# A convolution step ahead of the second pair's sums, and a bias made on GpSimd

## What is computed

```python
# block 0: bottleneck with a deformable 3 x 3 convolution
out = relu(group_norm(conv(x, w1)))                 # 256 -> 64 channels, 32 groups of 2
om = conv(out, w_off, pad=1) + b_off                # 27 rows: x and y offsets, mask
sampled = bilinear_sample(out, py, px) * sigmoid(om[:, 18:])
out = relu(group_norm(einsum(sampled, w2)))         # groups of 2 channels
x = relu(group_norm(conv(out, w3)) + x)             # 64 -> 256, groups of 8

# block 1: three convolutions on inputs rounded to 16 bits, weights to powers of two
h = shift_conv(x, w1)
h = relu(bn(shift_conv(h, peg_w, pad=1) + peg_b))
h = relu(bn(shift_conv(h, w2, pad=1)))
out = relu(bn(shift_conv(h, w3)) + x)
```

## Time and profile before

| what | us |
|---|---|
| median of 3 runs | 90.41 |
| the three runs | 89.57, 90.41, 90.43 |
| the profiled execution | 90.49 |
| its span, first to last instruction | 88.7 |
| mean granted TensorE clock in it | 0.990 |
| TensorE matmuls busy | 75.2 |
| VectorE busy | 65.4 |
| ScalarE busy | 50.1 |
| GpSimd busy | 5.0 |

### The profile page before, as it was taken

How to read it: one execution, slowest core, us unless ns; L and a number is a source line. 1 busy time by engine, 2 the same in 40 slices (tenths; PEclk the granted TensorE clock), 3 DMA queues, 4 the chain that set the end, 5 groups by cost and what they waited for, 6 DMA issues and landing times.

```text
span 88.7 us, 2177 instructions
## 1 busy us (share of the span) xinstructions
PE 75.2 (85%) x893; PEld 51.6 (58%) x893; DVE 65.4 (74%) x176; ACT 50.1 (56%) x89; POOL 5.0 (6%) x10
## 2 busy tenths in 40 slices
PE   5988999996899898999999999899589887779600
PEld 1333666475698797888988897345233374555400
DVE  0424539999999789999897725899896784967850
ACT  4203165679974999996868003906672254732660
POOL 7600110000000000000003100000000000000000
PEclk9999999999999999999999999999999999999995
DMA  1999800000000000000000000000000000000076
GB/s 30 326 317 313 346 12 0 7 0 0 0 7 0 0 7 0 4 11 0 0 7 0 0 0 7 0 0 0 0 0 0 0 0 0 0 7 4 5 258 211
DMA packets 3290, 4.17 MB, mean 47 GB/s; under 512 B 272, under 2 KB 2704, under 8 KB 3280
## 3 DMA queue, kind: packets, MB, share of 16 engines
q1 hardware_dynamic: 3008, 3.76, 13.0%
q10 hardware_dynamic: 272, 0.26, 0.9%
HBM read 2.98 MB, written 1.05 MB: 45 GB/s over the span
## 4 chain that ended last, share of the span: by engine, by line
PE 43%; DVE 31%; ACT 10%; DMA 6%; issue 4%; SPq 2%; DVEq 0%; ACTq 0%
PE acc L492 15%; PE slot L479 10%; DVE g_rows L926 9%; DMA x_sb<-x 6%; PE acc L624 4%; DVE g_cols L1028 3%; PE acc L603 3%; PE slot L407 3%; ACT g_cols L728 2%; PE slot L528 2%; ACT g_cols L826 2%; DVE g_cols L1074 2%; ACT pad L785 2%; PE slot L564 2%; DVE g_cols L1166 2%
## 5 line engine op out<-in xcount | busy, mean ns | idle before, releaser
L926 DVE TENSOR_TENSOR g_rows<-hats 128x2304 f32<-128x2304 f32 (+1 forms) x12 | 20.6, 1753 | 0.1
L728 ACT ACTIVATE g_cols<-slot 128x768 f32<-128x768 f32 x24 | 17.8, 829 | 3.7 <-PE slot L479 3.7
L492 PE MATMUL acc<-g_cols,v_sb 128*64 128x128 f32 x288 | 17.7, 276 | 0.0
L492 PEld LDWEIGHTS acc<-g_cols,v_sb 128*64 128x64 f32 x288 | 15.5, 137 | 1.1 <-issue 0.3
L370 PE MATMUL slot<-zeros 128*128 128x512 bf16 x54 | 15.0, 412 | 1.0 <-DVE zeros L845 1.0
L479 PE MATMUL slot<-consts_sb,g_rows 64*128 64x64 f32 x288 | 11.8, 226 | 2.1 <-DVE g_rows L926 1.7
L479 PEld LDWEIGHTS slot<-consts_sb,g_rows 64*128 64x128 f32 x288 | 10.3, 140 | 3.9 <-DVE g_rows L926 2.6
L370 PEld LDWEIGHTS slot<-zeros 128*128 128x128 bf16 x54 | 5.5, 109 | 6.9 <-issue 2.1
L785 ACT ACTIVATE pad<-g_cols 64x256 bf16<-64x256 int8 x8 | 3.3, 417 | 4.9 <-DVE g_cols L1074 4.8
L857 DVE BATCH_NORM_STATS2 stats<-acc 128x6 f32<-128x256 f32 x4 | 1.7, 430 | 4.1 <-PE acc L382 2.5
L407 PE MATMUL slot<-feat,woff_sb 128*64 128x256 f32 x36 | 4.7, 385 | 0.0
(11 more groups left out here) (141 smaller groups left out, 118.1 us busy)
## 6 DMA issues: line engine op xcount, KB each, us to landing
x_sb<-x SPq DMA_DIRECT2D x3, 256.0 KB, 4.5
out<-g_cols SPq DMA_DIRECT2D x3, 256.0 KB, 2.3
wq_sb<-wq SPq DMA_DIRECT2D x1, 484.5 KB, 6.3
woff_sb<-woff SPq DMA_DIRECT2D x1, 288.0 KB, 5.6
w_sb<-w SPq DMA_DIRECT2D x1, 288.0 KB, 5.5
x_sb<-x ACTq DMA_DIRECT2D x1, 256.0 KB, 2.9
w_sb<-w SPq DMA_DIRECT2D x1, 256.0 KB, 6.4
out<-g_cols SPq DMA_DIRECT2D x2, 128.0 KB, 1.8
```

Of the source, the lines that this page charges most:

```text
L492: mm = nc.tensor.matmul(acc[b2][rows(h), at:at + P], v_sb[:, B2 * h + b2, q, k, :], g_cols[t][h][:, NQ * k + q, :], start=(k == 0 and q == ...
L728: nc.scalar.activation(dst.rearrange("p k (r n) -> p k r n", r=HALVES), src.rearrange("p r (k n) -> p k r n", k=per), ACT.Copy).then_inc(g ...
L926: tt(g_rows[i % 3][:, taps], hats[:, t, h, 1, taps].unsqueeze(3).to_broadcast(shape), hats[:, t, h, 0, taps].unsqueeze(2).to_broadcast(sha ...
```

## The change

On TensorE the three idle matmuls before the second pair's sums are taken out. The first of the five steps of the first pair's offset convolution is put ahead of these sums, the other four behind them. In the second pair's convolution the turn of the first pair's offsets stands behind the first step instead of the second.

At the end of block 0 the bias of the second pair is made by two instructions on GpSimd instead of VectorE. The normalisation of the second pair multiplies by the scale only. The residual is added and the pieces' maxima are taken without the bias. The bias is added in the relu: on ScalarE in three instructions, one for each piece (a bias is one value per partition and piece), and on VectorE for the fourth piece. The overall maximum becomes: the first pair's four maxima first (in largest(0), ahead of that pair's relu), and at the end one operation that adds the bias to the second pair's four maxima and takes the greatest of them and of the first. The two kernels compute the same.

The diff, cut to its core:

```diff
             pair_sums(1, 0)
             conv1(1)
-            idle(IDLE[2], spare)
-            pair_sums(2, 1)
...
             pe.wait_ge(woff_in, 16)
-            for b2 in range(B2):
-                pe.wait_ge(feat_ready, b2 + 1)
-                for s in range(TAPS_A):
-                    mm = om_step(b2, s)
-                    if b2 == 1 and s == 1:
-                        pe.wait_ge(consts_in, 16)
-                        om_turn(0)
-                mm.then_inc(om_done, 1)
+            pe.wait_ge(feat_ready, 1)
+            for s in range(TAPS_A):
+                mm = om_step(0, s)
+                if s == 0:
+                    pair_sums(2, 1)
+            mm.then_inc(om_done, 1)
+            pe.wait_ge(feat_ready, 2)
+            for s in range(TAPS_A):
+                mm = om_step(1, s)
+                if s == 0:
+                    pe.wait_ge(consts_in, 16)
+                    om_turn(0)
+            mm.then_inc(om_done, 1)
+            pe.wait_ge(w2_in, 16)
...
+            pool.wait_ge(gn_ready, 11)
+            nc.gpsimd.tensor_tensor(dev_sb[:, 1, :], rstd[:, 1, :], mean_gamma[:, 1, :], ALU.mult).then_inc(dev_ready, 1)
+            pool.wait_ge(dev_ready, 1)
+            nc.gpsimd.tensor_tensor(gn_bias[:, 1, :], vec[:, V_GN3B:V_GN3B + CH * HALVES], dev_sb[:, 1, :], ALU.subtract
+                                    ).then_inc(gn_ready, 1)
...
-                a.wait_ge(gn_ready, 2 * (5 + b2))
+                a.wait_ge(gn_ready, 2 * (5 + b2) - b2)
                 for i in pieces3:
                     c, h = i // HALVES, i % HALVES
+                    bias = gn_bias[:, b2, i:i + 1] if b2 == 0 else zero_sb[:, 0:1]
...
-            def relu0(b2):
+            def relu0(b2, pieces3=(0, 1, 2)):
 
                 a.wait_ge(sum_ready, 4 * b2 + 4)
-                nc.scalar.activation(flat(y0[:, 0, b2]), flat(y0[:, 0, b2]), ACT.Relu).then_inc(relu_ready, 1)
+                if b2 == 0:
+                    nc.scalar.activation(flat(y0[:, 0, b2]), flat(y0[:, 0, b2]), ACT.Relu).then_inc(relu_ready, 1)
+                    return
+                a.wait_ge(gn_ready, 12)
+                for i in pieces3:
+                    piece = y0[:, i // HALVES, b2, i % HALVES, :]
+                    nc.scalar.activation(piece, piece, ACT.Relu, bias=gn_bias[:, b2, i:i + 1]).then_inc(relu_ready, 1)
...
                 tt(gn_scale[:, b2, :], rstd[:, b2, :], vec[:, V_GN3S:V_GN3S + CH * HALVES], ALU.mult
                    ).then_inc(gn_ready, 1)
+                if b2 == 1:
+                    return
...
                 dve.wait_ge(sum_ready, 4 * b2 + 4)
-                if b2 == B2 - 1:
-                    nc.vector.tensor_reduce(mx[:, 1, 0:1], piece_max[:].rearrange("p b i -> p (b i)"), AX_X, ALU.max
-                                            ).then_inc(max_ready, 1)
-
-                return ts(flat(y0[:, 1, b2]), flat(y0[:, 1, b2]), 0.0, None, ALU.max)
+                if b2 == 0:
+                    nc.vector.tensor_reduce(mx[:, 1, 1:2], piece_max[:, 0, :], AX_X, ALU.max)
+                    return ts(flat(y0[:, 1, b2]), flat(y0[:, 1, b2]), 0.0, None, ALU.max)
+                dve.wait_ge(gn_ready, 12)
+                nc.vector.tensor_tensor_reduce(unused[:, 0:CH * HALVES], piece_max[:, 1, :], gn_bias[:, 1, :], 1.0,
+                                               mx[:, 1, 1:2], ALU.add, ALU.max, mx[:, 1, 0:1]).then_inc(max_ready, 1)
+
+                return ts(y0[:, 1, b2, 1, :], y0[:, 1, b2, 1, :], gn_bias[:, b2, 3:4], 0.0, ALU.add, ALU.max)
```

More of the change, by code:

```diff
@@ L233, in build @@
         mean_done = sem("mean_done")
+        dev_ready = sem("dev_ready")
         var_ready = sem("var_ready")
@@ L420, in om_turn @@
                 mm.then_inc(omt_done, 1)
-            pe.wait_ge(woff_in, 16)
-            for b2 in range(B2):
-                pe.wait_ge(feat_ready, b2 + 1)
-                for s in range(TAPS_A):
-                    mm = om_step(b2, s)
-                    if b2 == 1 and s == 1:
-                        pe.wait_ge(consts_in, 16)
-                        om_turn(0)
-                mm.then_inc(om_done, 1)
             v_banks = [small[0], small[1], acc[0], acc[1]]
-            pe.wait_ge(w2_in, 16)
             def make_v(i):
@@ L452, in make_last_v @@
                                         w2_sb[rows(h), BANK:TAPS * CB], start=True, stop=True)
+            pe.wait_ge(woff_in, 16)
+            pe.wait_ge(feat_ready, 1)
[12 more added lines that the diff above has]
+            pe.wait_ge(w2_in, 16)
             for i in range(4):
@@ L746, in norm3 @@
             def norm3(b2, pieces3=(0, 1, 2)):
-                a.wait_ge(gn_ready, 2 * (5 + b2))
+                a.wait_ge(gn_ready, 2 * (5 + b2) - b2)
                 for i in pieces3:
                     c, h = i // HALVES, i % HALVES
+                    bias = gn_bias[:, b2, i:i + 1] if b2 == 0 else zero_sb[:, 0:1]
                     nc.scalar.activation(y0[:, c, b2, h, :], conv3_out(c, h, b2),
-                                         ACT.Identity, bias=gn_bias[:, b2, i:i + 1], scale=gn_scale[:, b2, i:i + 1]
+                                         ACT.Identity, bias=bias, scale=gn_scale[:, b2, i:i + 1]
                                          ).then_inc(norm3_ready, 1)
-            def relu0(b2):
+            def relu0(b2, pieces3=(0, 1, 2)):
                 a.wait_ge(sum_ready, 4 * b2 + 4)
-                nc.scalar.activation(flat(y0[:, 0, b2]), flat(y0[:, 0, b2]), ACT.Relu).then_inc(relu_ready, 1)
+                if b2 == 0:
[5 more added lines that the diff above has]
+                    nc.scalar.activation(piece, piece, ACT.Relu, bias=gn_bias[:, b2, i:i + 1]).then_inc(relu_ready, 1)
             def square4(b2):
@@ L1013, in norm3 @@
             def norm3(b2):
-                dve.wait_ge(gn_ready, 2 * (5 + b2))
-                ts(y0[:, 1, b2, 1, :], conv3_out(1, 1, b2), gn_scale[:, b2, 3:4],
-                   gn_bias[:, b2, 3:4], ALU.mult, ALU.add).then_inc(half_read, 1)
+                dve.wait_ge(gn_ready, 2 * (5 + b2) - b2)
+                if b2 == 0:
+                    ts(y0[:, 1, b2, 1, :], conv3_out(1, 1, b2), gn_scale[:, b2, 3:4],
+                       gn_bias[:, b2, 3:4], ALU.mult, ALU.add).then_inc(half_read, 1)
+                else:
+                    ts(y0[:, 1, b2, 1, :], conv3_out(1, 1, b2), gn_scale[:, b2, 3:4], None, ALU.mult
+                       ).then_inc(half_read, 1)
             def add_residual(b2, order):
@@ L1091, in _ @@
             whole(flat(quot[:, 0, 0]), 1)
-            dve.wait_ge(relu_ready, 2)
+            dve.wait_ge(relu_ready, 3)
             quotient(1, flat(quot[:, 0, 1]), flat(y0[:, 0, 1]))
+            dve.wait_ge(relu_ready, 4)
             quotient(1, flat(quot[:, 1, 1]), flat(y0[:, 1, 1]))
```

## The result

| | before | changed |
|---|---|---|
| median of 20 runs each, us | 90.41 (89.57 to 91.20) | 90.90 (90.18 to 94.33) |
| ratio | | 1.0048, 95% interval 1.0025 to 1.0071 |

The changed kernel is slower by 0.5%, 0.43 us by the ratio (90.41 x 0.0048). The forecast was a gain of 0.15 us, and the median of 90.90 lies just above the end of its range, 90.8. The change is smaller than the 1% that the chances speak of, but clear of no change, and on the other side. The ratios in this document, e13's excepted, leave out executions in which TensorE's clock was visibly disturbed, while the medians and ranges hold all; so for small differences the ratio counts.

What follows compares the result with a forecast made beforehand. The prediction took handovers spread over all engines as the bound, with ScalarE, led by TensorE's v products, late in the middle. Terms -0.02 and -0.13 gave -0.15 us, from the 90.41 median to 90.26, so 90.3; range 89.5 to 90.8.

Steps and rivals of the forecast that it cites:

- the 1% that the chances speak of: About 0.9 us, taken as what a measurement tells from no change; chances 0.10 faster, 0.86 within, 0.04 slower.
- part one: TensorE's start: three idle matmuls out, one offset convolution step ahead of the second pair's sums; -0.02 us, bounds -0.32 and +0.2.
- part two: Block 0's tail: second pair's bias moved to GpSimd and the relu; -0.14 up to the spread, -0.13 us after the relus.
- The reading of the middle: Sampling section: ScalarE, led by TensorE's v products, is late and VectorE has slack, so the end moves by the smaller gain.
- a change of 0.15: Offset convolution on TensorE: changing from a step to a full-array operation costs 0.15 us, perhaps no more than chance.
- The turn's new place: Second pair's convolution: turn 0.45 earlier but waiting 0.12, the other step 0.43 behind it; v at 15.07 instead of 15.09.
- the rival of the convolution's gain in full: Middle: sampling products pace it, so the convolution's 0.32 us arrives in full; -0.46 in all, 89.95 us, chance 0.20.
- the extra maximum: Tail, VectorE ahead of the scale: a maximum over the first pair's four values adds 0.07 us.
- the accumulating maximum: Tail, VectorE: the final maximum becomes an operation with accumulator and read-out, 0.22 instead of 0.16; +0.06 us, bounds 0 and +0.19.
- GpSimd late or in the way: Tail: bias late, +0.16 us net (90.6), or VectorE's four residual sums stretched, 0.4 us (90.7); chance 0.10.
- the nearer row: Tail: GpSimd's 256-column copy, 0.40 us, used to size its two bias instructions; twice that fits the 2.1 us cover.
- Weights late: Start: the offset convolution's weights land late and hold step 0 and all behind it; up to +0.54 us, 90.95, chance 0.10.

Runs made afterwards that it cites:

- e13: The changed kernel with the three idle matmuls put back behind the second pair's first convolution: 91.26 us, ratio 1.0109 to the kernel before.
- e1: The changed kernel again, as it is, for another profile: 90.87 us, ratio 1.0062 to the kernel before.
- e2: Only TensorE's part of the diff (idle matmuls out, step 0 ahead of the sums, turn behind one step) on the kernel before: 91.11 us, ratio 1.0053.
- e4: The kernel before with only the three idle matmuls ahead of the second pair's sums taken out: 90.38 us, ratio 0.9973.
- e10: Part one with the convolution's weights issued ahead of the second pair's x, and three idle matmuls ahead of that pair's first convolution: 91.35 us, ratio 1.0119 to before.
- e5: The kernel before, unchanged, as an experiment of its own: 90.43 us, ratio 1.0018.
- e9: The kernel before without its three idle matmuls, convolution weights issued ahead of the second pair's x, three idle matmuls ahead of its first convolution: 91.60 us, ratio 1.0138.
- e3: The diff without TensorE's part (bias on GpSimd and in the relu, start as before) on the kernel before: 90.27 us, ratio 0.9976.
- e8: Part two with the three idle matmuls taken out and the order of before: 90.24 us, ratio 0.9986 to the kernel before.
- e11: Part two alone once more, the same kernel as e3: 90.16 us, ratio 0.9949 to the kernel before.
- e14: The changed kernel a third time, as it is: 90.72 us, ratio 1.0033 to the kernel before.
- e6: Part one with the turn behind two steps of the second pair, as before: 90.88 us, ratio 1.0038 to the kernel before.
- e7: The kernel before without the three idle matmuls and with the turn behind one step, sums ahead of the whole convolution: 90.89 us, ratio 1.0020.
- e12: Part two without the three idle matmuls, order of before, once more (same kernel as e8): 91.34 us, ratio 0.9981 to the kernel before.

## Why the prediction was wrong

**The step that failed** is in part one: "The sums are a full-array operation too. They now start at 8.89 + 0.43 + 0.15 = 9.47 instead of 9.36, 0.11 later; bounds 0 (the 0.15 may be no more than chance) and 0.2." The sum on the left is nearly right: the sums start 0.63 behind the features in it and 0.73 in e1 and 0.72 in e2 (that e1's 9.51 is so near to 9.47 is in part luck, its features came 0.06 earlier). What is wrong is the 9.36 to which it is compared, and so the bound of 0.2: against e4, with the features at the same moment, e2's sums are 0.73 later, and v 0.63. So part one, forecast at -0.02 with +0.2 as the worst, cost 0.48 us (1.0053). The change puts the second pair's sums behind two things that they don't need, the first pair's features and step 0. What this costs depends on how far the moments lie behind the features. The working took 0.46 for it, from one execution, and never named it as a number that a load's landing sets.

Two sums describe the profiles of full clock in which neither x nor the weights held TensorE otherwise:

- old order: v starts 0.06 + 5.73 = 5.79 behind the second pair's moments;
- new order: step 0 starts 0.14 behind the first pair's features, the sums 0.59 behind step 0, and v 5.63 behind the sums, 6.36 in all behind the features. Where the moments come later than step 0, as in e10, it is 0.06 + 5.63 behind them.

| execution | features ready | moments ready | v by the sum | v in the trace |
|---|---|---|---|---|
| before | 8.84 | 9.30 | 15.09 | 15.09 |
| e5, old order | 8.73 | 8.77 | 14.56 | 14.56 |
| e4, old order | 9.33 | 9.26 | 15.05 | 15.05 |
| e9, old order, late x | 9.36 | 9.89 | 15.68 | 15.68 |
| e1, new order | 8.78 | 8.67 | 15.14 | 15.13 |
| e2, new order | 9.33 | 9.21 | 15.69 | 15.68 |
| e10, new order, late x | 9.36 | 10.15 | 15.84 | 15.84 |

The other profiles with a full clock there (e3, e8, e11, e13, e14) follow the same two sums to 0.01. The two are equal when the moments come 6.36 - 5.79 = 0.57 behind the features. Even the recorded execution, at 0.46, would have lost 0.1 us. And from 0.67 on, where the moments are later than step 0, the new order gains no more than 5.79 - 5.69 = 0.10. Of the thirteen other profiles with the loads in their old places two have late x, e6 at 0.50 and the disturbed one of the result. In the remaining eleven the moments come from 0.12 ahead to 0.04 behind, so part one costs 0.53 to 0.69 at v. The end follows v one for one: the span is v's start plus 73.6 in all profiles without part two that had their clock (before, e2, e4, e5, e6, e7, e9, e10), and plus 73.4 in those with it (e1, e3, e8, e11, e14). From these the changed kernel should lose about 0.6 - 0.2 = 0.4 us; measured were 0.43, 0.56 and 0.30 (the three ratios by 90.4).

**Right in part one.** A step of 0.43 and a change of 0.15 (together 0.58 to 0.59 in e1 and e2). The features of the first pair to step 0 took 0.14 instead of the 0.05 assumed, which is small. The reading of the middle holds. VectorE's chain did come 0.3 earlier relative to TensorE, and e1 shows where it went: into the wait at the third mask, 1.23 instead of 0.90. So TensorE's v products decide, as the prediction said, and the rival of the convolution's gain in full (89.95) is out. The turn's new place costs, as the prediction held. Had only the turn been wrong, e6 would have been at the time of before; it isn't.

**Right in part two, with small errors of size.** Forecast -0.13; by the two constants -0.2; timed -0.24% and -0.51%. The normalisation gained 0.26 (forecast 0.27), the extra maximum took 0.07 (0.07), the accumulating maximum 0.08 (0.06), and the relus ended just ahead of the quotients, 0.05 to spare (they were to be 0.01 late). Not priced was that VectorE's own normalisation, with a scale and no bias, takes 0.48 instead of 0.54, one row of the timeline of before and one of e1's:

```profile
61.45 0.54 DVE L1016 TENSOR_SCALAR g_cols<-slot,gn_scale,gn_bias 128x256 f32<-128x256 f32 x1
...
61.28 0.48 DVE L1035 TENSOR_SCALAR g_cols<-slot,gn_scale 128x256 f32<-128x256 f32 x1
```

**The rivals.** GpSimd late or in the way: out. Its two instructions took 0.20 each, as the nearer row would have it or better, the bias was ready 1.5 us ahead, and the four sums with the residual still stand 0.35 apart. The Trainium skill (Advanced Engine Details and Errata, GPSIMD Details) has GpSimd conflict with VectorE's instructions of two SBUF inputs; here GpSimd is done at 61.55 in e3, as the first of these sums starts, so the runs neither show nor exclude it. Weights late: it happens, in the profile that came with the result, and for e6 a wait of 0.47 ended by these weights stands ahead of step 0 (8.68, where the features at 8.40 would have let it start at 8.54); in e1, e2 and e10 step 0 waits for the features. It was the rival with the right sign and not the cause: e2's step 0 waits on ScalarE, and loses 0.6 all the same. The rule cited from the Trainium skill (TensorE: Matmul & The Clock Gate, Part 3: Packing small matmuls), that full-row weights can't load beside a step in flight, speaks against the change and agrees with the 0.15, but explains only this part of the 0.73.

**Open.** What the removed idle matmuls cost through the clock. The prediction counted nothing for them, on the strength of one wait of 1.01 in one execution. Counted over the runs, 33 of 116 executions without the three ahead of the second pair's sums (the changed kernel, e2, e4, e6, e7, e8, e12) lie above 91.5 us, all with a mean granted clock below 0.98, and 13 of 177 with them (the kernel before, e3, e11). In the result it is 6 of 20 against none, which the ratio of 1.0048 doesn't hold. The share is higher without them on each chip on which both ran. So the nothing was probably wrong too, and this cost comes on top of the one explained above. It isn't shown as a cause: e12 fell to half after a gap and e4 did not after the same gap, and e13, with the three back but ahead of step 0, had three of only six. Why the second pair's x lands later in some executions was not tried.

**The better version** is part two alone, with the order and the idle matmuls of before: ratio 0.9976 (its interval holds 1) and 0.9949 (its interval doesn't), the first against the same runs of before by which the changed kernel stood at 1.0062 and part one at 1.0053.

## What to carry to other kernels

When an instruction is moved ahead of another on an in-order engine, write down what each of the two waits for, and price the case in which the one that is pushed back is ready first. If the two are fed by different loads, their distance in one profile is a draw and not a property of the kernel: look at it in several executions, or state the break-even distance (0.57 us here) and bound the price from both sides of it. Where idle matmuls are taken out, look also at how many executions lose their clock, and not at one profile. A forecast can hit every moment of the new schedule, as this one did, and still have the wrong sign because the moment it subtracts was unusual.

## What the runs showed of the hardware that was not expected

- The same kernel's loads land half a microsecond apart from one execution to the next: the second pair's moments at 9.30 in the profile of before and at 8.77 in e5, and the convolution's weights 5.3 us from issue in e1 and 6.9 in the profile that came with the result. This is more than what the change does.
- GpSimd takes 0.20 us for an elementwise instruction of 128x4 and starts a dependent second one 0.27 behind the first (61.33 and 61.60 in e1). VectorE takes 0.17 and 0.16 for such a one. The slower engine costs nothing here, since 1.5 us lie between its result and the use of it.
- The granted clock fell to 0.50 of full speed from 10.5 to 13.5 us in e12, where TensorE had stood for 0.77 us before 9.34, and stayed at full speed in e4, e7 and e8, which have a gap of 0.75 to 0.78 at the same place. In e13 it fell to 0.63 (24 to 26 us) and 0.51 (26 to 28) behind a gap of 0.85, and in e1 it stayed full behind the same gap.
